# Two-layer graph network, second edge loop: two raw first pairs in buffers of their own, and the nodes' own part dealt out over the first four pairs

## The reference, cut to what matters

```python
h = jnp.maximum(_layernorm(x), 0.0)                      # x: rows after the first layer ("x1")
em = concat([h[src], h[dst]]) @ msg_w + msg_b            # one row per edge
em = relu(layer_norm(em, msg_g, msg_beta)) * edge_weight
messages = segment_sum(em, dst) / counts
gate  = sigmoid(h @ gate_w + gate_b)
h_new = relu(layer_norm(concat([h, messages]) @ upd_w + upd_b, upd_g, upd_beta))
out   = x + gate * h_new + (1 - gate) * h
```

## Time and profile before

| | us |
|---|---|
| median of 3 runs | 2334.95 (2334.86 to 2338.51) |
| the profiled execution, its time | 2336.42 |
| its span, first to last instruction | 2334.6 |
| POOL busy | 1629.6 (70%) |
| PE busy, PEld busy | 1625.3 (70%), 1208.7 (52%) |
| DVE busy | 1545.5 (66%) |
| ACT busy | 1040.7 (45%) |

### The profile page before, as it was taken

How to read it: one execution, slowest core, us unless ns; L and a number is a source line. 1 busy time by engine, 2 the same in 40 slices (tenths; PEclk the granted TensorE clock), 3 DMA queues, 4 the chain that set the end, 5 groups by cost and what they waited for, 6 DMA issues and landing times.

```text
span 2334.6 us, 44737 instructions
## 1 busy us (share of the span) xinstructions
PE 1625.3 (70%) x9949; PEld 1208.7 (52%) x10012; DVE 1545.5 (66%) x5047; ACT 1040.7 (45%) x3865; POOL 1629.6 (70%) x1709
## 2 busy tenths in 40 slices
PE   5587787777877778787476667766667666766663
PEld 4365555555655556465365555554545444544542
DVE  7666665656565565555778877767666666767658
ACT  6344444333434344344454554444444444434437
POOL 6677777777777777776047777777777777777740
PEclk9799998999899898989588888878887888888876
DMA  8644444434444444443553444444343434344432
GB/s 220 183 98 95 91 94 94 92 88 94 87 96 89 93 93 89 93 88 72 162 162 74 94 94 95 95 94 92 88 93 86 92 87 94 87 93 92 90 96 62
DMA packets 207931, 231.83 MB, mean 99 GB/s; under 512 B 102692, under 2 KB 151990, under 8 KB 207807
## 3 DMA queue, kind: packets, MB, share of 16 engines
q0 software_dynamic: 55168, 114.83, 25.6%
q1 hardware_dynamic: 151232, 115.62, 17.8%
q10 hardware_dynamic: 1472, 0.73, 0.2%
HBM read 194.58 MB, written 36.44 MB: 99 GB/s over the span
## 4 chain that ended last, share of the span: by engine, by line
POOL 41%; issue 18%; PE 13%; DMA 12%; DVE 10%; SPq 3%; ACT 2%; POOLq 1%; DVEq 0%; ACTq 0%
POOL room L702 41%; DMA room<-src_table,rec 4%; DMA state<-st_out 4%; PE psum L853 2%; PE psum L835 2%; DMA room<-dst_perm 2%; PE psum L818 2%; PE psum L825 1%; PE psum L921 1%; DMA st_in<-state 1%; PE psum L926 1%; DVE stats L1325 1%; PE psum L939 1%; DMA room<-in_edge_weight 1%; PE psum L752 1%
## 5 line engine op out<-in xcount | busy, mean ns | idle before, releaser
L702 POOL DMA_INDIRECT room<-src_table,rec x1638 | 1574.5, 961 | 523.8 <-issue 488.1
L921 PE MATMUL psum<-room,ident 128*128 128x384 f32 (+1 forms) x512 | 296.1, 667 | 326.4 <-DMA room<-src_table,rec 241.7
L1205 ACT ACTIVATE room<-psum 128x128 f32<-128x128 f32 x832 | 219.4, 275 | 519.4 <-DVE room L1747 518.6
L1560 DVE TENSOR_TENSOR room<-psum,room 128x384 f32<-128x384 f32 (+1 forms) x256 | 151.0, 590 | 373.0 <-ACT room L1137 245.4
L1137 ACT ACTIVATE room<-psum 128x384 f32<-128x384 f32 (+1 forms) x256 | 131.7, 514 | 523.8 <-PE psum L825 508.6
L1747 DVE TENSOR_TENSOR room<-psum,msg_g 128x384 f32<-128x384 f32 (+1 forms) x256 | 150.2, 587 | 256.1 <-PE psum L926 249.8
L939 PE MATMUL psum<-room 128*125 128x128 f32 x1664 | 273.7, 309 | 11.4 <-ACT room L1217 11.4
L926 PEld LDWEIGHTS psum<-room 125*128 125x128 bf16 x2496 | 201.4, 114 | 149.3 <-issue 128.3
L921 PEld LDWEIGHTS psum<-room,ident 128*128 128x128 f32 x512 | 93.9, 229 | 347.1 <-issue 291.3
L853 PE MATMUL psum<-room 128*125 128x128 f32 x1664 | 259.8, 298 | 18.2 <-ACT room L1155 13.6
L1761 DVE SCALAR_TENSOR_TENSOR room<-room,rstd_e,msg_beta 128x128 f32<-128x128 f32 x832 | 242.6, 348 | 10.2
(11 more groups left out here) (223 smaller groups left out, 2221.0 us busy)
## 6 DMA issues: line engine op xcount, KB each, us to landing
room<-dst_perm SPq DMA_DIRECT2D x128, 406.2 KB
room<-src_table,rec POOLq DMA_INDIRECT x1638
room<-dst_table SPq DMA_DIRECT2D x128, 62.5 KB
src_table<-rows SPq DMA_DIRECT2D x24, 224.0 KB
dst_table<-rows SPq DMA_DIRECT2D x24, 224.0 KB
st_in<-state SPq DMA_DIRECT2D x64, 64.0 KB
state<-st_out SPq DMA_DIRECT2D x64, 64.0 KB
st_in<-state SPq DMA_DIRECT2D x64, 62.5 KB
```

Of the source, the lines that this page charges most:

```text
L702: pool.indirect_dma_start(out=xg[:, u, t * P:(t + 1) * P], out_offset=None, in_=table[:, :], in_offset=bass.IndirectOffsetOnAxis(ap=rec[:, ...
L921: nc.tensor.matmul(msg_bank[b][:, cols], ident[:, :], xg[:, u, t0 * P:t1 * P], start=True, stop=False, skip_group_check=True)
L1205: i = nc.scalar.activation(sq[:, j * P:(j + 1) * P], msg_bank[b][:, j * P:(j + 1) * P], ACT.Square, accum_out=var_e[:, c, j:j + 1])
```

## The change

Four things, all but the first in the second loop:

1. Raw pairs get buffers `raw_xg` and `raw_xg2` and their own places of `rec` (4 and 5) beside the ring. The first loop has one such pair as before, the second has two. A gather into a ring place that a raw pair would have used no longer waits for PE, only for that raw pair's own gather. SP loads the `rec` of the pair after a raw one without waiting for PE's reading of it.
2. In the second loop pairs 0 and 1 gather from `x1_rows`; POOL waits for the stored source table before pair 2.
3. The own part is cut in 17 groups of 3 node tiles. Groups 0 and 1 stand before the raw pairs, 2 to 4 after them, and 5 to 16 in the slots of pairs 0 to 3, one in each of blocks 0, 1 and 2: `update_own` on PE after `msg_message`, `gate_of` and `own_rest` on ACT after `msg_squares`, `own_part` on DVE one block later, after `msg_norm`.
4. 1 - gate is a second sigmoid on ACT, and relu(h) * rest moves from DVE to ACT (`own_rest`, three activations with a scale per row); DVE's `own_part` keeps two of its four instructions.

```diff
+RAW = (1, 2)
+NGX = NG + RAW[0] * NB
+OWN = [(t, min(t + 3, NT)) for t in range(0, NT, 3)]
+NOWN = len(OWN)
...
+        raw_xg = sb("raw_xg", [P, CH])
+        rec = sb("rec", [P, U + 2, 3 * T])
+        raw_xg2 = take(CH)
...
+        def rows_in(s, k, u):
+            if is_raw(s, k):
+                return (raw_xg, raw_xg2)[k]
+            return xg[:, u, :]
...
@@ sync, feed
                     if there(k, -3, end):
-                        ge(sp, s.m, nth(k - 1, NB))
-                        settle(sp)
-                        if n == 1:
-                            ge(sp, s.pm, 2 * k)
+                        if is_raw(s, k - 1):
+                            sp.wait_ge(s.rec[(u + 3) % U], turns(s, k - 1, (u + 3) % U, U, 16, last))
                             settle(sp)
+                        else:
+                            ge(sp, s.m, nth(k - 1, NB))
+                            settle(sp)
+                            if n == 1:
+                                ge(sp, s.pm, 2 * k)
+                                settle(sp)
                         load_rec(sp, s, k + 3, (u + 3) % U)
...
@@ gpsimd
-                table = (a["x"], x1_rows)[n] if type(k) is int and k == 0 else src_table[n]
+                table = (a["x"], x1_rows)[n] if is_raw(s, k) else src_table[n]
...
-                    if type(k) is not int or k >= U:
+                    if type(k) is int and k >= U and is_raw(s, k - U):
+                        pool.wait_ge(s.xg[u][b], turns(s, k - U, u, U, 16 * (t1 - t0), last))
+                    elif type(k) is not int or k >= U:
...
-                if type(k) is int and k == 1:
+                if type(k) is int and k == RAW[1]:
                     tables_stored(1)
...
@@ tensor
+        OWN_AHEAD, OWN_FIRST = 2, 5
+        OWN_AT = [(k, b) for k in range(U) for b in range(NB - 1)]
...
+        def own_bank(g):
+            return banks[4 + g % 2][0:PP, 0:3 * (D + 1)].rearrange("p (i f) -> p i f", f=D + 1)
...
             def msg_slot(k, u, end):
                 for b in range(NB):
                     if there(k, 0, end):
                         msg_message(k, u, b)
+                    if own_group(k, b) is not None:
+                        update_own(own_group(k, b))
                     lagged(msg_sums, k, u, b, 3, end)
...
+            for g in range(OWN_AHEAD):
                 update_own(g)
+            for r in range(RAW[1]):
+                raw_pair(pe, msg, r, msg_wc)
+            for g in range(OWN_AHEAD, OWN_FIRST):
+                update_own(g)
...
@@ scalar
                         msg_squares(k, u, b)
+                    if own_group(k, b) is not None:
+                        gate_of(own_group(k, b))
+                        own_rest(own_group(k, b))
                     lagged(msg_relu, k, u, b, 1, end)
...
+                nc.scalar.activation(gate[:, t0:t1], own_bank(g)[:, 0:t1 - t0, D], ACT.Sigmoid, bias=gate_b[0:PP, :])
+                nc.scalar.activation(rest[:, t0:t1], own_bank(g)[:, 0:t1 - t0, D], ACT.Sigmoid, bias=gate_nb[0:PP, :],
+                                     scale=-1.0).then_inc(s_gate, 1)
+
+            def own_rest(g):
+                t0, t1 = OWN[g]
+                act.wait_ge(s_gate, g + 1)
+                for t in range(t0, t1):
+                    i = nc.scalar.activation(node_h[:, t, :], node_h[:, t, :], ACT.Relu, scale=rest[:, t:t + 1])
+                i.then_inc(s_keep, 1)
+
+            for g in range(OWN_AHEAD):
                 gate_of(g)
+            for g in range(OWN_AHEAD):
+                own_rest(g)
+            raw_pair(msg, 0)
             split_high(msg, 0, 0)
+            raw_pair(msg, 1)
             split_mid(msg, 0, 0)
+            for g in range(OWN_AHEAD, OWN_FIRST):
+                gate_of(g)
+                own_rest(g)
...
@@ vector
+            tables(1, msg_b, {NG - NB + 1 + b: lambda b=b: raw_stats_of(msg, 0, b) for b in range(NB - 1)})
+            raw_stats_of(msg, 0, NB - 1)
+            raw_scale(1, 0)
...
-                dve.wait_ge(s_gate, g + 1)
-                dve.tensor_scalar(rest[:, t0:t1], gate[:, t0:t1], -1.0, 1.0, ALU.mult, ALU.add).then_inc(s_rest, 1)
-                dve.wait_ge(s_rest, g + 1)
-                dve.scalar_tensor_tensor(out=node_h[:, t0:t1, :], in0=node_h[:, t0:t1, :], scalar=0.0,
-                                         in1=rest[:, t0:t1].unsqueeze(2).to_broadcast([PP, nt, D]), op0=ALU.max,
-                                         op1=ALU.mult).then_inc(s_held, 1)
-                dve.wait_ge(s_held, 2 * g + 1)
+                dve.wait_ge(s_keep, g + 1)
                 dve.tensor_tensor(node_x[:, t0:t1, :], node_x[:, t0:t1, :], node_h[:, t0:t1, :], ALU.add).then_inc(s_held, 1)
...
-            for g in range(NG):
+            for g in range(OWN_AHEAD):
                 own_part(g)
-                if g in RAW_ROWS:
-                    raw_rows(1, RAW_ROWS.index(g), msg_b)
+            for b in range(NB):
+                raw_stats_of(msg, 1, b)
+            raw_scale(1, 1)
+            for b in range(NB):
+                raw_rows(msg, 0, b, msg_b)
...
                     lagged(msg_norm, k, u, b, 1, end)
+                    if own_group_back(k, b) is not None:
+                        own_part(own_group_back(k, b))
...
             msg_relative(0, 0)
-            split_rest(msg, 0, 0)
             one_hot(msg, 0, 0)
-            split_low(msg, 0, 0)
             msg_prob(0, 0, 0)
             msg_prob(0, 0, 1)
+            split_rest(msg, 0, 0)
+            for b in range(NB):
+                raw_rows(msg, 1, b, msg_b)
+            split_low(msg, 0, 0)
+            for g in range(OWN_AHEAD, OWN_FIRST):
+                own_part(g)
             all_pairs(dve, msg_slot, last, 1)
```

More of the change, by code:

```diff
@@ L408, in block_count, with all_pairs @@
                                   skip_runtime_bounds_check_because="it follows from the count of pairs")
-        def all_pairs(eng, slot, last, tail):
-            for k in range(U):
-                slot(k, k, None)
-            with eng.Fori(U, last, U) as k:
+        def all_pairs(eng, slot, last, tail, ahead=U):
+            for k in range(ahead):
+                slot(k, k % U, None)
+            with eng.Fori(ahead, last, U) as k:
                 for u in range(U):
@@ L871, in _ @@
             pe.wait_ge(s_row, NG)
[L872 to L876 removed]
+            raw_pair(pe, gat, 0, w_lr)
             pe.wait_ge(s_weout, 32)
```

216 lines of the change are left out of this document (109 added, 107 removed).

## The result

| | before | after |
|---|---|---|
| time, median | 2335.22 us (2334.86 to 2338.51, 4 runs) | 2350.97 us (2349.15 to 2352.88, 4 runs) |
| ratio to before | | 1.0071 (95% interval 1.0059 to 1.0083) |
| profiled execution, its span | 2336.4, 2334.6 us | 2352.9, 2351.0 us |

The account below looks back on a forecast made before the run. POOL was taken to bound the kernel, held by `rec` at the compute engines' pace. Pair 7 at T + 86.1 + 9.1 = 1332.7 against 1314.2 moves the end 18.5 us, from 2334.95 to 2353.5 us; likeliest case's range 2340 to 2370.

Parts of the forecast that it names:

- POOL bounds, by its permission to gather: Second loop: POOL's instructions are 41% of the chain; the question is when it may issue gathers, at most three pairs ahead.
- some 35: Sign of being right: POOL waits for `rec` at pairs 5, 6 and 7, in sum some 35 us.
- The 9.1 us from `split_low` of pair k to pair k + 3: POOL cannot begin pair k + 3 earlier than 9.1 us after DVE's `split_low` of pair k, through SP's store and `rec`.
- POOL's side: Pair 1 gathers from x1 in idle time, 1192.7 to 1208.9; pair 2 begins about 1211.4; 16.3 us to win.
- T: When PE begins pair 0 of the second loop: 1237.5, 7.8 us earlier than before.
- the 1.5 us for DMA contention: Term in T: pair 1's gathers share the DMA engines with the table stores; 1.5 us added, bounds 0 and 4.
- A pair with own groups: Pairs 1 to 4, one `split_low` to the next: 21.4 us, 8.5 more than before, set by ACT with five table loads.
- The sum: POOL's pair 5 not before 1289.9, pair 6 1311.3, pair 7 1332.7; the end 18.5 us later, 2353.5 us; chance 0.80.
- Own parts at no cost: Rival: own parts fill ACT's holes in the slots, a pair stays at 12.9 us, time 2327; chance 0.08.
- DVE's pace: Rival: table loads overlap waits, a pair takes 16.4 us, pair 7 begins 1.0 us earlier, time 2334; chance 0.09.
- the 16.7 at which the change begins to lose: Time of a pair with own groups, 16.7 us, from which the change makes the kernel slower.
- A switch at twice the row: Rival: each ACT table load has another 1.28 us around it, 21 loads, 27 us, time 2380; chance 0.03.

Follow-up runs that it names:

- The run without switches: Changed kernel with loop bounds asserted, the sigmoids of own groups 5 to 16 replaced by relus so ACT needs no other table in the slots: 2337.97 us, ratio 1.0016.
- the last run: Changed kernel with all gate columns made by one-column products behind the messages of pairs 0 and 1, own groups in pairs 1 to 7: 2329.52 us, ratio 0.9975.
- gates once: Changed kernel with all gate columns made by one-column products ahead of the loop, own groups 1 to 16 two to a pair: 2338.42 us, ratio 1.0015.

## Why the prediction was right

*POOL bounds, by its permission to gather.* Right. The three waits for `rec` at pairs 5, 6 and 7 sum to 35.8 us, "some 35" on record, and no wait over 0.3 us came in the loop's middle or on PE's `m`. The 9.1 us from `split_low` of pair k to pair k + 3 held for pair 5 in eight kernels (8.8 to 9.4), but not as a rule for every pair: it is 8.6 us for pair 6 and 10.7 us for pair 7, which is the one that sets the end. The trace before has `rec` of pair 7 8.0 us behind `split_low` of pair 4, so this could have been read; the prediction read slot 2 alone.

*POOL's side.* Right: pair 1 at 1192.3 (1192.7), pair 2 at 1212.7 (1211.4).

*T.* 1235.8, predicted 1237.5, by the working that was given: raw pair 0's normalization begins on ACT at 1214.7 (1213.0), the raw pairs' relus are done at 1222.7 and 1230.7 (1221 and 1230.4). Three terms were off and in part cancel: PE's own groups 0 and 1 took 2.9 us and not 1.7; raw pair 1 with its root took ACT 8.0 us and not 9.4; and of the 1.5 us for DMA contention 0.9 show, by which the tables' last group is later than in the earlier trace rows:

```profile
1206.62 0.75 DVE L1402 TENSOR_TENSOR rows<-psum,msg_b 125x256 f32<-125x256 f32 x2 [0.15 <-DMA dst_table<-rows]
```

*A pair with own groups.* 21.2 us, predicted 21.4, and for the reason given. There were 28 table loads, as counted (1 at the root of raw pair 0, 14 for sigmoids, 13 for roots), and the 25 in the slots stand back to back with their neighbours. The run without switches shows that they are the cause.

*The sum.* Pair 5 at 1286.8 (1289.9), pair 6 at 1307.7 (1311.3), pair 7 at 1330.4 (1332.7). Of the 3.1 us over at pair 5, T has 1.7 and slot 0, 21.0 us to `split_low` instead of 21.9, has 0.9; the shift was 16.2 us where 18.5 was on record, and the end followed pair 7 within 0.2 us. That pair 7 is off by 2.3 us only is in part luck: T was 1.7 us over and the four pairs 2.2 us (T + 83.9 instead of T + 86.1), while the last step was 1.6 us under, 10.7 us instead of 9.1.

*The rivals.* Own parts at no cost would have needed 12.9 us a pair. DVE's pace of 16.4 us a pair was low for the case without switches: measured 17.6 on average (1253.25 to 1305.91, three pairs), above the 16.7 at which the change begins to lose; and that kernel was indeed 0.16% slower than before, with T 1.1 us under the predicted one. A switch at twice the row, the rival with 2380, did not come. The Trainium skill, page "ScalarE: Activation LUTs", section "What ACT_TABLE_LOAD costs", has the load at ~1283 ns, which is the mean here, and a drain of ~1380 ns beside it, which does not show: 25 loads in the stretch have 0.4 us of idle time before them in all. The advice of the same page of the Trainium skill, section "Table sets: the hidden batching unit", is to batch activations by table set; the last run fits it, with two switches there and back where the change has one in each of twelve blocks.

What the prediction did not see is that either half of the change, alone, loses nearly as much as both. It priced the dealt-out groups as the loss, and with one raw pair they do lose (2348.13 us). But the second raw pair with all groups first takes the same time as the changed kernel (2351.58 us), since the groups then cost 27 us in T; that run keeps the own part's new form, whose share is not shown.

## What to carry to other kernels

Where the bounding engine works ahead through a ring and through lists that another queue loads late, its end is that of the last place where it is held: find that place, trace it back to the pace of the others, and price every change there; a wait 19 us shorter was worth 4 to 9 us here. Read the way to every held pair, not to one: it was 9 us long at pair 5 and 11 at pair 7. Work moved out of a prologue into a loop that "has time" must be priced by what it puts into the chain of a slot, on an engine with function tables above all by its switches: gather what needs the other table into one or two instructions. And the same extra work costs more or less by where it stands in an engine's queue. 2 x 25 small products took 16.8 us in front of the raw pairs; moved behind the messages, with the own group that stood ahead of the loop, they left T 11.6 us earlier, and held pair 1 up by 3.7 us and pair 2 by 1. The two kernels are 9 us apart; the products were not moved alone.

## What was not expected of the hardware

- A product's price here is hardly its width; it goes with the granted clock. From start to start, 25 tiles of a one-column product, 50 passes, took 5.6 us (0.112 us a pass) at a granted clock of 0.98 in the last run, and 6 passes of 128 columns beside them 0.71 us (0.118) at 1.00. PEld, the weight load, was busy for the whole of that one-column pass. The same 50 passes took 6.5 us at 0.83, 8.0 at 0.66 and 10.1 at 0.52. The slowest, from 1206.2 to 1216.2 us in "gates once", had PE busy without a hole; from 1195 to 1205 us, before it, the clock was 1.00 with PE busy 8.4 of 10 us on products of 125 to 256 columns.
- Nothing of a drain before or after a table load on ACT: at each of 25, the instruction before ends and the one behind begins within 0.01 to 0.02 us of the load.
- On two occasions all kernels ran a third longer, the kernel before too (3091 and 3093 against 2335 us), with equal busy times of DVE, ACT and POOL, PE at 1847.7 instead of 1613.3 us busy at a mean granted clock of 0.78 instead of 0.87, and on POOL 101 waits of 2.3 us on average whose releaser the profile gives as `remote`. It is not a matter of one chip: the second occasion and the last run, where the kernel before took 2334.84 us, were on the same one. What it is stays open.
